# Some exps of an attention layer on VectorE, ahead of their turn, and no GpSimd beside it

## What is computed

```python
h = _layernorm(x, axis=-1) * (1 + ca) + sa
# attention, 16 heads of 16 features: q = h Wq by head, keys and values are q itself
scores = jnp.einsum('bnhe,bmhe->bhnm', q, q) / NORM
attn = jax.nn.softmax(scores, axis=-1)
res = jnp.einsum('bhnm,bmhe->bnhe', attn, q)
x = x + ga * (res.reshape(B, N, D) @ Wp.T + bp)
h = _layernorm(x, axis=-1) * (1 + cb) + sb
# feed-forward: layernorm with gamma and beta, 256 -> 1024, silu, 1024 -> 256, weights stored as integers with scales
x = x + gb * ffn(h)
```

## Time and profile before

| | |
|---|---|
| median of 3 runs | 2083.67 us (2083.09 to 2083.87) |
| the profiled execution | 2083.57 us, its span 2081.8 us |
| ScalarE busy | 1970.0 us (95%), 1894.6 of it in 2048 exps |
| TensorE busy | 1960.0 us (94%) |
| VectorE busy | 377.9 us (18%) |
| GpSimd busy | 70.4 us (3%) |
| mean granted TensorE clock | 0.992 |

### The profile page before, as it was taken

How to read it: one execution, slowest core, us unless ns; L and a number is a source line. 1 busy time by engine, 2 the same in 40 slices (tenths; PEclk the granted TensorE clock), 3 DMA queues, 4 the chain that set the end, 5 groups by cost and what they waited for, 6 DMA issues and landing times.

```text
span 2081.8 us, 42098 instructions
## 1 busy us (share of the span) xinstructions
PE 1960.0 (94%) x18325; PEld 535.0 (26%) x18325; DVE 377.9 (18%) x903; ACT 1970.0 (95%) x2174; POOL 70.4 (3%) x35
## 2 busy tenths in 40 slices
PE   5888889999999999999999999999999999999996
PEld 4311112222222222222222222222222222222223
DVE  7310002210041100410022100311004100231004
ACT  3899999999999999999999999999999999999982
POOL 0000000100010000100001000100001000010000
PEclk9899999999999999999999999999999999999998
DMA  4541111211111111111211111111111111111100
GB/s 159 149 123 46 35 50 42 49 51 42 54 40 46 51 50 51 46 44 41 56 46 50 51 41 55 36 50 51 48 53 44 46 42 56 46 40 41 31 11 12
DMA packets 121337, 108.05 MB, mean 52 GB/s; under 512 B 21936, under 2 KB 120112, under 8 KB 120896
## 3 DMA queue, kind: packets, MB, share of 16 engines
q1 hardware_dynamic: 120400, 103.69, 18.4%
q10 hardware_dynamic: 752, 1.67, 0.2%
HBM read 96.49 MB, written 8.65 MB: 51 GB/s over the span
## 4 chain that ended last, share of the span: by engine, by line
ACT 59%; PE 27%; issue 10%; DVE 1%; ACTq 0%; DVEq 0%
ACT attend_probs L744 58%; PE attend_sums L788 14%; PE attend_scores L776 7%; PE attend_out L796 4%; PE attend_scores L796 1%; PE attend_out L802 1%; ACT attend_half_tanh L729 1%; ACT attend_ffn_in L753 0%; PE attend_scores L802 0%; DVE attend_st L1085 0%; DVE z L1097 0%; PE attend_sums L802 0%; DVE attend_rsqrt_work L93 0%; DVE attend_rsqrt_work L91 0%; DVE attend_rs L95 0%
## 5 line engine op out<-in xcount | busy, mean ns | idle before, releaser
L744 ACT ACTIVATE attend_probs<-attend_scores 128x1024 f32<-128x1024 f32 x2048 | 1894.6, 1038 | 25.1 <-PE attend_scores L776 25.1
L788 PE MATMUL attend_sums<-attend_probs,values 128*17 128x512 f32 x8192 | 1011.2, 597 | 0.0
L776 PE MATMUL attend_scores<-asks,keys 64*128 64x512 f16 x4096 | 674.7, 384 | 81.8 <-ACT attend_probs L744 62.3
L776 PEld LDWEIGHTS attend_scores<-asks,keys 64*128 64x128 f16 x4096 | 151.5, 94 | 896.4 <-ACT attend_probs L744 819.9
L788 PEld LDWEIGHTS attend_sums<-attend_probs,values 128*17 128x17 f32 x8192 | 171.7, 96 | 390.6 <-issue 388.3
L796 PE MATMUL attend_out<-w,hidden 128*32 128x256 f32 x1920 | 124.2, 379 | 0.0
L796 PE MATMUL attend_out<-attend_ffn_in,w 128*32 128x512 f32 x896 | 116.6, 592 | 0.0
L927 DVE COPY attend_sums_sb<-attend_sums 128x512 f32<-128x512 f32 x32 | 22.1, 692 | 488.1 <-PE attend_sums L788 488.1
L991 DVE TENSOR_SCALAR attend_half_in<-attend_out,b_col 128x512 f32<-128x512 f32 x56 | 42.0, 751 | 339.9 <-PE attend_out L796 338.9
L796 PEld LDWEIGHTS attend_out<-w,hidden 128*32 128x32 f32 x1920 | 62.0, 110 | 86.4 <-issue 64.3
L1001 DVE TENSOR_TENSOR base<-attend_out,base 128x512 f32<-128x512 f32 x14 | 9.7, 691 | 377.2 <-PE attend_out L796 377.2
(11 more groups left out here) (140 smaller groups left out, 548.9 us busy)
## 6 DMA issues: line engine op xcount, KB each, us to landing
keys<-parts_dram SPq DMA_DIRECT2D x768, 64.0 KB
keys<-parts_dram SPq DMA_DIRECT2D x256, 56.0 KB
asks<-parts_dram SPq DMA_DIRECT2D x192, 64.0 KB
start_x_in<-L_attn_x SPq DMA_DIRECT2D x8, 512.0 KB, 9.5
parts_dram<-start_q_parts SPq DMA_DIRECT2D x16, 256.0 KB, 2.5
attend_x_now<-L_attn_x SPq DMA_DIRECT2D x8, 512.0 KB, 4.5
out<-base SPq DMA_DIRECT2D x16, 256.0 KB, 2.6
asks<-parts_dram SPq DMA_DIRECT2D x64, 56.0 KB
```

What stands on the lines that cost most here:

```text
L744: act.activation(probs[n % P_RING], ps_scores[:, 2 * slot:2 * slot + 2, :], ACT.Exp, scale=scale)\
L776: last = pe.matmul(ps_scores[:, 2 * (n % S_RING) + b, :], keys[rows, part % K_RING, hq, col:col + P], asks[rows, group * Q_HEADS + hq, :], ...
L788: last = pe.matmul(ps_sums[32 * hq:32 * hq + E1, :], values[:, j + STEPS * b, (gg % Q_GROUPS) * Q_HEADS + hq, :], probs[n % P_RING][:, b, ...
```

## The change

`emission()` writes out a new order of the pairs. In certain rounds (`vector_round`) the first place goes to the pair that stands 12 places further on (`LEAD`), and VectorE takes its exps. All other pairs keep their order among themselves and fill the remaining places; ScalarE takes those. These are 164 pairs of 2048. `ORDER`, `PLACE` and `TURN` say which pair stands where, and how many of its kind stand before it. Slots of PSUM still go by place, three in turn. A slot that VectorE has read is free at `taken`, after the first of seven steps.

The seven steps (`exp_step`), each on 128 x 1024 elements: scale the scores to units of the exponent and write them as integers; keep the mantissa bits as a fraction; keep the exponent bits and put a factor in with an exclusive or; then four steps with two tensors each, which evaluate a quartic as a product of two quadratics and multiply by the power of two. Steps 0 to 2 stand in the round of the pair, 3 and 4 in the next one, 5 and 6 in the one after, written into VectorE's list, which now goes round by round. There are two buffers for the results (`E_RING`), one of the powers, one of the fraction. To make room, `hid` now shares the buffer of `z1`, and x is loaded straight into `x1`.

The weighing of a step waits for the scalar pairs and the vector pairs in it. GpSimd's four instructions a chunk move to VectorE: `add_bias` in round 4 of group 0, the product in `second_norm`, `finish_base` in round 9 of group 2. `weights` and `gate_weights` move to rounds 8 and 12 of group 1. SP loads x and stores y in part 14.

```diff
+LEAD, E_RING = 12, 2
+def vector_round(gg, r):
+    if gg < Q_GROUPS:
+        return r % 3 == 0 and (gg != 1 or r not in (6, 9, 12)) and r < 21
+    busy = gg % Q_GROUPS == 0 and 11 <= r <= 18
+    return (len(SIZES) * gg + r) % 4 == 0 and not busy
+def emission():
+    order, by_vector, taken, following = [], [], set(), 0
+    for gg in range(GROUPS):
+        for r in range(len(SIZES)):
+            for i in range(SIZES[r]):
+                early = len(order) + LEAD
+                if i == 0 and vector_round(gg, r) and early < GROUPS * PAIRS and early not in taken:
+                    order.append(early)
+                    by_vector.append(True)
+                    taken.add(early)
+                    continue
+                while following in taken:
+                    following += 1
+                order.append(following)
+                by_vector.append(False)
+                taken.add(following)
+    return order, by_vector
...
-        z2 = z1
+        hid = z2 = z1[:, :, :]
...
-                    if within == 8 and c > 0:
-                        sp.wait_ge(x1_ready, 2 * c)
+                    if within == 14 and c > 0:
+                        sp.wait_ge(base_step, 3 * c)
                         load_x(sp, c)
...
+                        if not BY_VECTOR[e]:
+                            turn, slot = TURN[e], e % S_RING
+                            act.wait_ge(scores_ready, e + 1)
+                            if turn >= P_RING:
+                                act.wait_ge(steps_done, SCALAR_PAIRS[turn - P_RING] // Q_HEADS + 1)
+                            act.activation(probs[turn % P_RING], ps_scores[:, 2 * slot:2 * slot + 2, :], ACT.Exp, scale=scale)\
+                               .then_inc(exps_done, 1)
...
-                    wait(pe, exps_done, n - S_RING + 1)
+                    if e >= S_RING:
+                        pe.wait_ge(taken if BY_VECTOR[e - S_RING] else exps_done, TURN[e - S_RING] + 1)
...
-                        pe.wait_ge(exps_done, gg * PAIRS + Q_HEADS * (j + 1))
+                        pe.wait_ge(exps_done, before(SCALAR_PAIRS, gg * PAIRS + Q_HEADS * (j + 1)))
+                        wait(pe, vector_exps, before(VECTOR_PAIRS, gg * PAIRS + Q_HEADS * (j + 1)))
...
+                    if i == 0:
+                        dve.wait_ge(scores_ready, e + 1)
...
+                        dve.tensor_scalar(power, ps_scores[:, 2 * slot:2 * slot + 2, :].rearrange("p b n -> p (b n)"),
+                                          log2_scale, -120.0 * 2.0 ** 23, ALU.mult, ALU.max).then_inc(taken, 1)
+                    elif i == 1:
...
+                        dve.tensor_scalar(fraction.bitcast(I32), power, 0x007FFFFF, 0x3E800000,
+                                          ALU.bitwise_and, ALU.bitwise_or).then_inc(power_step, 1)
+                    elif i == 2:
...
+                        dve.tensor_scalar(power, power, 0x7F800000, FACTOR,
+                                          ALU.bitwise_and, ALU.bitwise_xor).then_inc(power_step, 1)
+                    elif i == 3:
...
+                        if d >= E_RING:
+                            dve.wait_ge(steps_done, VECTOR_PAIRS[d - E_RING] // Q_HEADS + 1)
+                        dve.scalar_tensor_tensor(out=values_out, in0=fraction, scalar=A1 * 2.0 ** -2, in1=fraction,
+                                                 op0=ALU.add, op1=ALU.mult).then_inc(power_step, 1)
...
                 for gg in range(GROUPS):
                     c, group = divmod(gg, Q_GROUPS)
...
+                    for r in range(len(SIZES)):
+                        now = len(SIZES) * gg + r
+                        if r % 2 == 0 and c > 0 and (r > 0 or group > 0):
+                            after_piece(c - 1, group * SLOTS + r // 2 - 1)
+                        if BY_VECTOR[gg * PAIRS + STARTS[r]]:
+                            exps_at[now] = exps_begun
+                            exps_begun += 1
+                            for i in (0, 1, 2):
+                                exp_step(exps_at[now], i)
+                        if r == 0 and gg > 0:
+                            copy_sums(gg - 1)
+                        if r == 1 and gg > 0:
+                            divide(gg - 1)
+                        if now - 1 in exps_at:
+                            for i in (3, 4):
+                                exp_step(exps_at[now - 1], i)
+                        if now - 2 in exps_at:
+                            for i in (5, 6):
+                                exp_step(exps_at[now - 2], i)
+                        if r % 2 == 1 and c > 0:
+                            s = group * SLOTS + r // 2 - 1
+                            if s > 0:
+                                after_tanh(c - 1, s)
...
+                        if (group, r) == (0, 4) and c > 0:
+                            add_bias(c - 1)
+                        if (group, r) == (2, 9) and c > 0:
+                            finish_base(c - 1)
```

144 lines of the change are left out of this document (87 added, 57 removed).

## The result

The changed kernel takes 2123.08 us, the median of four runs (2121.01 to 2124.09), against 2083.77 for the kernel before: a ratio of 1.0188 with a 95% interval of 1.0176 to 1.0201, so 39 us or 1.9% slower. Its profiled execution took 2121.01 us, its span 2119.2; that span is 37.4 longer than the span before. This was the fastest of the four, so the trace accounts for some 2 us less than the medians do.

What follows compares the result with a forecast made beforehand. The prediction took two loops of ScalarE and TensorE latencies as the bound. Terms 8.7+10.4+6.6+3.7+6.3+3.5+0.2=39.4 us on 2083.6 gave 2123 us, range 2100 to 2150.

Steps and rivals of the forecast that it cites:

- two loops of latencies: ScalarE and TensorE tied through even and through odd rounds, 5.50 us per two rounds; even-round pairs shorten only one.
- the signs: Expected in the trace: ScalarE busy some 150 us less, idle on scores up as much, weighing waits some 40 us.
- The waits for exps just scored: TensorE's weighing asks for exps of its own round: group ends 8.7 and 10.4, round 3 6.6, round 20 3.7 us.
- the boundaries: First weighing of each later group stalls 0.75, or 0.98 with a vector pair there: 8.7 and 10.4 us in all.
- round 3: First weighing unit in odd groups of later chunks stalls 0.75, of which 0.47 arrives: 14 times, 6.6 us.
- round 20: Second unit in a TensorE-bound round of two pairs waits for its exp: 14 x 0.10 + 7 x 0.33, 3.7 us.
- VectorE's work: Seven instructions a pair, 7.8 us with bit steps at 0.68, about 1280 us in all; pace held in later groups.
- The rival that VectorE becomes the bound: Bit steps at 1.225 or more gaps, 8.9 us a pair: about 2147 us, chance 0.25.
- The divide: Steps 5 and 6 delay the divide at the next group's start; TensorE stands 0.45 in round 2: 14 times, 6.3 us.
- take_up held back: On VectorE, delayed by a divide (7 x 0.2) or finish_base (7 x 0.3), with a tanh and exps behind: 3.5 us.
- The first four groups: Start 1.7, boundaries 1.8 and VectorE late at round 3 4.2, against 7.5 gained from odd vector rounds: +0.2 us.
- elsewhere the wait falls on the second unit: Other step ends weighed in their own round: wait ends within 0.05, taken at 0, at most 1.8 us.

Runs made afterwards that it cites:

- first experiment: Changed kernel with LEAD=0, so pairs stay in their own place, and only the PSUM read left on VectorE, those pairs' exps left out: 2072.82 us.
- either parity alone: Read-only pairs, none ahead of turn, exps left out, against the changed kernel: in later groups even rounds only, 2072.82 us, or odd rounds only, 2112.19 us.
- both together: Changed kernel, read-only pairs in their own places, even and odd rounds from the fifth group on, none during the norms, exps left out: 2032.37 us.
- the twins: Changed kernel cut to 63 full vector pairs, LEAD=11: in odd rounds 2047.55 us; every pair one round earlier, in even rounds, 2058.72 us.
- three buffers: Changed kernel, LEAD=12 kept, only VectorE's PSUM read left, exps of its pairs left out, three result buffers instead of two: 2114.30 us.
- The experiment that turned the two round: Changed kernel with steps 5 and 6 of a round 20 pair put behind the next group's divide: 2132.07 us in a single run.
- the two kernels with the trap: Changed kernel, read-only pairs in their own places, later groups, not kept away from the norms: odd rounds 2112.19 us, odd and even rounds 2133.79 us.
- both parities: Changed kernel, read-only pairs in their own places, even and odd rounds from the fifth group on, not kept away from the norms: 2133.79 us.

## Why the prediction was right

**The bound.** The step on which all rests, two loops of latencies, of which the even rounds' pairs shorten only one, is shown: 140 pairs off ScalarE in even rounds give 6 us (first experiment), either parity alone gives a group without tanh at most 0.2, both together 1.05, and 14 pairs of the first four groups give 0.7 each in odd rounds and at most 0.3 a group in even ones (the twins). Of the signs, ScalarE's busy time fell by 126 us where I had named 150. The rest goes with the gaps: 1884 exps cover 1768.9 us, 0.939 each, where 2048 covered 1894.6, 0.925 each, since an exp behind a gap doesn't overlap the one before it. Its idle time on scores rose from 25.1 to 178.6 us, as named.

**The waits for exps just scored.** Right in kind, and at the boundaries in size: a stall of 0.97 (predicted 0.98) and 0.75 (0.75). The order alone makes them (2114.3 with three buffers). The sign that I had named for them was wrong: some 40 us in 50 to 60 places, against 157.1 in 196. By the emission rule 195 ends of steps fall into the round in which they are weighed, 52 of them at a round's first unit; I had put down only those that I thought would cost time, while the row shows all. Within the later chunks, round 3 measured 0.57 for 0.47 and round 20 0.26 for 0.10: the cover that I subtracted, TensorE's lead from a vector pair in round 2 and the slack of a short round, was smaller than I put it.

**VectorE's work.** The first, the last and the second of the seven steps, after:

```profile
L1060 DVE TENSOR_SCALAR attend_power<-attend_scores,gains 128x1024 int32<-128x1024 f32 x164 | 210.0, 1280 | 202.1 <-PE attend_scores L828 185.6 <-issue 16.5
...
L1087 DVE SCALAR_TENSOR_TENSOR attend_exps<-attend_exps,attend_fraction 128x1024 f32<-128x1024 f32 x164 | 200.9, 1225 | 5.6
...
L1065 DVE TENSOR_SCALAR attend_fraction<-attend_power 128x1024 int32<-128x1024 int32 x164 | 113.8, 694 | 5.7
```

It is 0.694 for the bit steps, 0.68 predicted from the 0.415 row (at the pace of the two rows 0.415+0.25=0.665); 1.280 and 1.225 as taken. The rival that VectorE becomes the bound rested on 1.225 for them, and fell with it. The Trainium skill, VectorE: DVE Perf Modes, section on the perf-mode tier table, is agreed with here: it gives fp32 `tensor_scalar` in SBUF twice the pace of a two-tensor instruction, and integer work with one source took 0.694 us against 1.225 with two tensors. That isn't quite half, but from 512 to 1024 elements the time grows from 0.415 to 0.694, so part of it doesn't grow with the size.

**The divide.** Right in place and count, 0.27 for 0.45. What was mis-sized is the start: I had the reciprocal at 3.4 after round 1's scores, and it came at 3.14 (889.08-885.94; 0.92 later than in the earlier trace rows, not 1.25), since step 5 starts 0.08 before the copy ends and the reciprocal 0.09 before step 6 does. The copy itself ends 0.83 after the scores, as before, and the third score of round 2 comes at 3.34 (predicted 3.35). The experiment that turned the two round shows that this order doesn't avoid the price.

**take_up held back** isn't in the trace: no round of the changed kernel's later groups shows it. The term was mis-sized by its whole 3.5. Why the room was larger than I gave it stays open.

**The first four groups** are the real miss, +6.2 for +0.2. The step that failed is "elsewhere the wait falls on the second unit and ends within 0.05 of it: taken at 0". It is wrong in two ways. First, in all four groups the second unit of round 4, and in three of them that of round 16, ask for the second exp of their own round, not the first. This takes away the gain of rounds 3 and 15: of 11 odd vector rounds at 0.68 only four gain, 0.77 each. That VectorE's lateness isn't what takes round 3's gain is shown by the kernel with three buffers, where VectorE has only the read and the gain is gone all the same. Second, the first unit of round 19 asks for its own round's exp, a stall of 0.6 that my list of step ends doesn't have; two rounds of two pairs follow, bound by TensorE, and give nothing back. (Round 7 has the same stall of 0.60 in three groups and gives it back in round 8.) VectorE's lateness at round 3 itself was predicted rightly: 1.4, and the changed kernel loses 1.36 more there than the kernel with three buffers. Round 3 itself, group 2 after:

```profile
215.17 1.23 DVE L1087 SCALAR_TENSOR_TENSOR attend_exps<-attend_exps,attend_fraction 128x1024 f32<-128x1024 f32 x1
216.31 1.28 DVE L1060 TENSOR_SCALAR attend_power<-attend_scores,gains 128x1024 int32<-128x1024 f32 x1
...
217.64 0.33 PEld L828 LDWEIGHTS attend_scores<-asks,keys 64*128 64x128 f16 x6 [2.37 <-DVE attend_power L1060]
...
220.07 0.13 PEld L841 LDWEIGHTS attend_sums<-attend_probs,values 128*17 128x17 f32 x8 [1.54 <-ACT attend_probs L790]
```

Step 6 (215.17) ends at 216.40, the read starts at 216.31, and the scores that need its slot wait 2.37. It is named and placed as predicted, but with the gain gone it costs 1.31 net for 0.72 a time.

## What to carry to other kernels

Where two engines are both near 95%, look for the loop of latencies that ties them together before taking work off either; work that leaves an engine where it shortens only one of two loops of equal length is worth next to nothing (0.2 us a group here), and a few items in the right rounds are worth more than many in the wrong ones. A reordering has to be priced by what it pushes back as well as by what it brings forward: list for each consumer how far ahead its newest input is made. A total that comes out right proves no term; only terms read one by one from the traces, or runs of the halves, do.

## What was not expected of the hardware

Two VectorE instructions that don't depend on each other overlap by 0.08 to 0.09 us (copy ends 886.77, step 5 starts 886.69), while dependent ones stand 0.03 apart (step 5 ends 887.91, step 6 starts 887.94).

A stand of TensorE can cost more than its length. In the two kernels with the trap the granted clock fell to 0.5 while TensorE stood, 7 us in the one and 14.5 in the other, and stayed there for 6.8 to 10.2 and for 13.7 to 17.1 us, of which 2.7 to 6.1 lie behind the end of the stand. The round behind the stand (round 16) then lasted 4.1 to 5.0 us where it lasts 3.6 before, and with both parities round 13 lasted 3.0 to 3.2 for 1.9. The 7.7 to 8.8 and 13.3 to 14.8 us by which these groups were longer hold both.

The prediction asked if VectorE's small instructions would get shorter without GpSimd's work. They did: the one of 4 elements that averaged 1203 ns takes 170 ns in all 14 places after. The average hid two values, 0.17 and some 2.2 us. Before, one of the long ones beside GpSimd:

```profile
364.98 2.39 POOL L717 TENSOR_TENSOR base<-base,b_gb 128x1024 f32<-128x1024 f32 x1
...
365.16 2.23 DVE L88 TENSOR_SCALAR attend_rs<-attend_rsqrt_work 128x4 int32<-128x4 int32 x1
```

It starts 0.18 behind GpSimd's instruction and ends 0.02 behind its end (367.39, 367.37). The same instruction at 356.57, with GpSimd idle, takes 0.17. That GpSimd holds it up is what these times suggest; no run changes that alone.
